# Attention and a look-up FFN on one core: context scaled by reciprocal sums instead of normalised probabilities, weights looked up bit by bit

## The reference

```
xn = layernorm(x)
q, k, v = split(xn @ qkv_w + qkv_b)                  # 16 heads of 128
scores = q @ k.T + alibi_mask                        # causal, slope 2**(-head/2), no 1/sqrt(d)
attn = softmax(scores);  ctx = attn @ v
attention = ctx @ out_w + out_b
gate, up = xn @ lut[gate_idx].T, xn @ lut[up_idx].T  # lut has 16 values, 688 x 256 codes each
ffn = (silu(gate) * up) @ lut[down_idx].T
out = x + attention + ffn
```

## Time and profile before

| | |
|---|---|
| median of three runs | 544.28 us (542.76 to 547.27) |
| the profiled execution: its own time | 543.26 us |
| its span (first to last instruction) | 541.5 us |
| mean granted TensorE clock | 0.987 of full speed |
| busy: PE / PEld / DVE / ACT / POOL | 493.8 / 422.4 / 414.2 / 360.9 / 403.6 us |
| one steady pair of heads | 57.0 us, six of them |
| last pair's end and FFN (from 440 us on) | 101.5 us |

### The profile page before, as it was taken

How to read it: one execution, slowest core, us unless ns; L and a number is a source line. 1 busy time by engine, 2 the same in 40 slices (tenths; PEclk the granted TensorE clock), 3 DMA queues, 4 the chain that set the end, 5 groups by cost and what they waited for, 6 DMA issues and landing times.

```text
span 541.5 us, 9700 instructions
## 1 busy us (share of the span) xinstructions
PE 493.8 (91%) x2826; PEld 422.4 (78%) x2826; DVE 414.2 (76%) x1067; ACT 360.9 (67%) x657; POOL 403.6 (75%) x312
## 2 busy tenths in 40 slices
PE   7896797999889988998899989997999989789998
PEld 6785576898779876987689768986798779578897
DVE  6796988788888878888788987888788886543541
ACT  3575867687767867595959685877678766824430
POOL 5533989788978998798969897889789979921400
PEclk9997999999999999999999999999999999979999
DMA  8204243332514070606160524134331514000001
GB/s 285 87 0 101 62 98 103 73 91 53 146 44 116 13 186 4 156 0 161 38 144 16 119 80 113 47 79 120 70 90 43 119 38 104 0 1 2 0 21 58
DMA packets 18948, 41.65 MB, mean 77 GB/s; under 512 B 4848, under 2 KB 7024, under 8 KB 18800
## 3 DMA queue, kind: packets, MB, share of 16 engines
q1 hardware_dynamic: 18928, 41.40, 30.2%
HBM read 11.83 MB, written 1.05 MB: 24 GB/s over the span
## 4 chain that ended last, share of the span: by engine, by line
POOL 44%; PE 23%; issue 21%; DVE 7%; ACT 3%; DMA 1%; POOLq 0%; DVEq 0%; ACTq 0%
POOL p_t_lo L1125 17%; POOL w_ffn L1153 15%; POOL work L1118 5%; PE ps_u L447 5%; PE ps_u L449 4%; PE ps_u L448 4%; DVE term L958 3%; PE ps_s L447 2%; PE ps_s L448 2%; PE ps_s L449 2%; POOL v_w_lo L1102 2%; POOL pad L1117 2%; POOL qk_w_lo L1097 2%; ACT ctx_t_hi L721 1%; DVE ctx_t_lo L898 1%
## 5 line engine op out<-in xcount | busy, mean ns | idle before, releaser
L1153 POOL TENSOR_TENSOR w_ffn<-w_ffn,term 128x1088 f32<-128x1088 f32 x60 | 155.0, 2584 | 45.4 <-DVE term L958 45.4
L1125 POOL TENSOR_TENSOR p_t_lo<-p_t_lo,p_t_hi 128x1024 fp32r<-128x1024 f32 (+2 forms) x60 | 133.1, 2251 | 0.0
L738 ACT ACTIVATE work<-work,neg_max 128x128 f32<-128x128 f32 (+7 forms) x128 | 99.0, 773 | 24.1 <-DVE neg_max L937 22.1
L937 DVE CUSTOM_DVE_ANT_0 work<-ps_s,alibi 128x128 f32<-128x128 f32 (+7 forms) x128 | 95.8, 749 | 0.0
L447 PE MATMUL ps_u<-p_t_hi,v_hi 128*128 128x512 f32 x192 | 70.5, 367 | 17.7 <-POOL p_t_lo L1125 17.4
L975 DVE STREAM_TRANSPOSE blocks<-work 128x512 f32<-128x512 f32 x120 | 65.3, 582 | 11.6 <-ACT work L750 11.6
L447 PE MATMUL ps_s<-k_hi,q_hi 128*128 128x256 f32 (+2 forms) x192 | 67.3, 350 | 5.3 <-DVE neg_max L937 5.3
L958 DVE TENSOR_SCALAR term<-codes,entry,table 128x1088 f32<-128x1088 uint8 x60 | 65.8, 1096 | 4.3 <-POOL w_ffn L1153 4.3
L449 PE MATMUL ps_u<-p_t_hi,v_lo 128*128 128x512 f32 x192 | 67.2, 350 | 0.0
L448 PE MATMUL ps_u<-p_t_lo,v_hi 128*128 128x512 f32 x192 | 67.0, 349 | 0.0
L448 PE MATMUL ps_s<-k_lo,q_hi 128*128 128x256 f32 (+2 forms) x192 | 65.8, 343 | 0.0
(11 more groups left out here) (148 smaller groups left out, 1271.1 us busy)
## 6 DMA issues: line engine op xcount, KB each, us to landing
p_t_lo<-blocks SPq DMA_DIRECT2D x240, 116.0 KB, 2.3
qk_raw<-w_qk SPq DMA_DIRECT2D x16, 256.0 KB, 2.7
w_ffn<-idx SPq DMA_DIRECT2D x1, 2176.0 KB, 11.0
v_raw<-w_v SPq DMA_DIRECT2D x8, 256.0 KB, 3.5
o_raw<-w_o SPq DMA_DIRECT2D x8, 256.0 KB, 2.9
out<-acc SPq DMA_DIRECT2D x8, 128.0 KB, 1.7
acc<-x SPq DMA_DIRECT2D x2, 256.0 KB, 3.0
acc<-x SPq DMA_DIRECT2D x1, 512.0 KB, 5.0
```

The source lines that it names most:

```text
L738: act.activation(slot(i), slot(i), ACT.Exp, bias=neg_max[:, col:col + 1], scale=-1.0, accum_out=row_sum[:, col:col + 1]).then_inc(exp_done, 1)
L937: dve.tensor_tensor_reduce(slot(i).rearrange("p (b c) -> p b c", b=banks), made_of, alibi[:, p, S - width:S].rearrange("p (b c) -> p b c", ...
L1125: pool.tensor_tensor(rows, rows.bitcast(F32), chunk_rows(0, chunk).bitcast(F32), ALU.subtract).then_inc(upper_lo, 1)
L1153: pool.tensor_tensor(piece, piece, term[:, :], ALU.add).then_inc(term_added, 1)
```

## The change

1. The probabilities stay unnormalised. `norm` is gone from ACT and POOL. DVE takes the reciprocals of four row sums at a time (`invert`, two per head instead of eight). SP writes these 128 x 4 numbers to a row of 512 in DRAM and reads the row back onto all 128 partitions (`send_inv`, `spread_inv`), twice a head. DVE multiplies the finished context by them (`scale`, in the place of its lo part), ACT then adds the bias and, in a second pass, makes hi, and POOL makes lo (`ctx_lo_of`).
2. The look-up works head by head on 272 codes (`PART`), all entries at once. DVE extracts four bits (`split_codes`, step 0). ACT fills a 128 x 8 x 272 buffer with the even table entries (`fill_codes`, end of step 0). DVE then picks with four predicated copies in steps 1 to 4, of 2176, 1088, 544 and 272 elements (`pick`), and ACT keeps the 272 results (`keep_codes`, step 5). POOL's sums are gone.
3. To make room, the weights of q and k have one buffer, and those of v and of the output share a raw one. The weights of the next head are now converted at step 2, after k1, and the units nk0 and nq0, which read them, go to steps 4 and 5. _out0 and _out1 go to 2 and 6.
4. The halving of the mask table goes from DVE (step 3) to POOL (step 5). The upper hi and lo parts start a step earlier (steps 3 and 4), and the upper blocks are turned one by one in steps 5 to 7. PE waits for `ctx_lo` before _out0 and _out2.

```diff
-QK_W_AT = 6
-V_W_AT = 2
+QK_W_AT = 2
+V_W_AT = 4
...
-ALIBI_AT = 3
...
+ALIBI_AT = 5
+HI_AT = {3: (0, 1), 4: (2, 3)}
...
     STEADY: [
-        (("q1", 0), ("k1", 1), ("nk0", 2), ("_out0", 3), ("nq0", 4), ("_out1", 5), ("_pv1-", 7), ("_pv1", 7),
+        (("q1", 0), ("k1", 1), ("_out0", 2), ("nk0", 4), ("nq0", 5), ("_out1", 6), ("_pv1-", 7), ("_pv1", 7),
          ("v0", 7), ("v1", 7)),
-        (("q1", 0), ("k1", 1), ("nk0", 2), ("_pv0", 2), ("v2", 3), ("nq0", 4), ("_out2", 4), ("v3", 5),
+        (("q1", 0), ("k1", 1), ("_pv0", 2), ("v2", 3), ("nk0", 4), ("_out2", 4), ("nq0", 5), ("v3", 5),
          ("_out3", 6), ("_pv1-", 7), ("_pv1", 7), ("pv0", 7)),
     ],
...
-        qk_w = [sb(f"qk_w_{s}", [P, 2, KT, 2 * D], F32R) for s in ("hi", "lo")]
+        qk_w = [sb(f"qk_w_{s}", [P, KT, 2 * D], F32R) for s in ("hi", "lo")]
...
+                sp.dma_start(inv_row[half].rearrange("(t q) -> q t", q=P),
+                             inv_sum[:, col:col + QT], allow_slow_non_contiguous=True).then_inc(inv_out, 16)
...
+                sp.dma_start(inv_rows[:, half, :], inv_row[half].partition_broadcast(P)).then_inc(inv_in, 16)
...
+            def upper_half(n, p):
+
+                send_inv(n, p, 1)
+                move(n, p)
+                spread_inv(n, p, 1)
...
                     if c == 0:
                         pe.wait_ge(o_w_hi, n)
                         pe.wait_ge(o_w_lo, n)
-                        pe.wait_ge(unit_used, number(n - 1, STEADY, 1, "pv0"))
+                        pe.wait_ge(ctx_lo, 16 * half_no(n - 1, 1, 0))
...
+                if "pv" in name:
+                    act.wait_ge(unit_used, no)
+                    rows = inv_rows[:, int(name[-1]), :]
+                    act.activation(rows, rows, ACT.Identity, bias=b).then_inc(ctx_biased, 1)
+                    act.wait_ge(ctx_biased, head)
+                    act.activation(unit_place(0, p, name), rows, ACT.Copy).then_inc(unit_hi, 1)
+                    return
...
+                evens = table[:, :].rearrange("p (c b) -> p c b", b=2)[:, :, 0:1]
+                act.activation(picked[:, :, :], evens.to_broadcast([P, PAIR_CODES, PART]),
+                               ACT.Copy).then_inc(codes_filled, 1)
...
+                        if i == 0:
+                            fill_codes(n, kind, p)
+                        if i == 5:
+                            keep_codes(n, p)
...
-                        if i == QK_W_AT and kind != LAST:
-                            act.wait_ge(qk_landed, n * 32 + (p + 3) * 16)
+                        if i == QK_W_AT and not (kind == LAST and p == 1):
+                            act.wait_ge(qk_landed, n * 32 + (p + 2) * 16)
                             act.wait_ge(unit_done, last_of(n, kind, p, "q1", "k1"))
...
+            def scale(n, p, name, bank, no, head):
+
+                c = int(name[-1])
+                dve.wait_ge(unit_done, no)
+                dve.wait_ge(inv_in, 16 * head)
+                dve.tensor_tensor(inv_rows[:, c, :], ps_u[:, bank, :], inv_rows[:, c, :],
+                                  ALU.mult).then_inc(unit_used, 1)
...
+                for bit in range(4):
+                    last = dve.tensor_scalar(bits[:, bit, :], codes, 1 << bit, None, ALU.bitwise_and)
+                last.then_inc(bits_made, 1)
...
+                count = PAIR_CODES // apart
+                dve.copy_predicated(out, bits[:, bit:bit + 1, :].to_broadcast([P, max(count, 1), PART]),
+                                    other).then_inc(codes_picked, 1)
...
+                        if i == 0:
+                            split_codes(n, kind, p)
+                        if 1 <= i <= 4:
+                            pick(n, kind, p, i - 1)
```

More of the change, by code:

```diff
@@ L340, in ffn_w @@
             if piece < 4:
[L341 removed]
+                room = (qk_w, v_w)[piece - 2][part]
+                return room[:, :, :].rearrange("p a b -> p (a b)")[:, in_piece:in_piece + width]
             in_piece += (piece - 4) * PIECE
@@ L386, in _, with send_inv, spread_inv @@
             sp.dma_start(bias[:, :, :], b_qkv).then_inc(bias_landed, 16)
[L387 removed]
+            sp.dma_start(vo_raw[:, :, :], w_v[0]).then_inc(v_landed, 16)
             sp.dma_start(table[:, :], lut.partition_broadcast(P)).then_inc(small_landed, 16)
[L389 removed]
+            sp.dma_start(out_bias(), b_out.partition_broadcast(P)).then_inc(small_landed, 16)
             sp.dma_start(w_ffn[:, :].bitcast(I32), idx).then_inc(idx_landed, 16)
[L391 to L395 removed]
+            sp.wait_ge(qk_w_hi, 1)
+            sp.wait_ge(qk_w_lo, 1)
+            sp.dma_start(qk_raw[:, :, :], w_qk[1]).then_inc(qk_landed, 16)
             sp.wait_ge(v_w_hi, 1)
             sp.wait_ge(v_w_lo, 1)
[L398 removed]
+            sp.dma_start(vo_raw[:, :, :], w_o[0]).then_inc(o_landed, 16)
+            def send_inv(n, p, half):
+                no = half_no(n, p, half)
+                before = 16 * no - 32
+                sp.wait_ge(inv_ready, no)
+                if not (isinstance(no, int) and no <= 2):
+                    sp.wait_ge(inv_in, before)
+                col = p * NT + half * QT
+                sp.dma_start(inv_row[half].rearrange("(t q) -> q t", q=P),
+                             inv_sum[:, col:col + QT], allow_slow_non_contiguous=True).then_inc(inv_out, 16)
+            def spread_inv(n, p, half):
+                no = half_no(n, p, half)
+                sent, before = 16 * no, 16 * no - 32
+                sp.wait_ge(inv_out, sent)
+                if not (isinstance(no, int) and no <= 2):
+                    sp.wait_ge(ctx_lo, before)
+                elif half == 1:
+                    sp.wait_ge(based, NT)
+                sp.dma_start(inv_rows[:, half, :], inv_row[half].partition_broadcast(P)).then_inc(inv_in, 16)
             def move(n, p):
@@ L667, in _ @@
                     if no in (0, 2):
-                        pe.wait_ge(unit_used, units)
+                        pe.wait_ge(ctx_lo, 16 * half_no(PAIRS - 1, 1, no // 2))
                     units += 1
@@ L836, in _ @@
                     if what == "pv":
-                        hi_of(PAIRS, 0, "_pv1", (units - 1) % 2, units)
+                        hi_of(PAIRS, 0, "_pv1", (units - 1) % 2, units, half_no(PAIRS - 1, 1, 1))
                         ffn_w_hi_of(4)
@@ L963, in invert, with turn_blocks @@
+            def invert(n, p, half):
+                dve.wait_ge(exp_done, tile_no(n, p, half * QT + QT - 1) + 1)
+                no = half_no(n, p, half)
+                if not (isinstance(no, int) and no <= 4):
+                    dve.wait_ge(inv_out, 16 * no - 64)
+                col = p * NT + half * QT
+                dve.reciprocal(inv_sum[:, col:col + QT], row_sum[:, col:col + QT]).then_inc(inv_ready, 1)
+            def turn_blocks(n, p, i):
                 dve.wait_ge(exp_done, tile_no(n, p, i) + 1)
-                col = (p * NT + i) % (2 * NT)
@@ L1011, in pair @@
                             if not (kind == FIRST and p == 0):
+                                if not kind == FIRST:
+                                    dve.wait_ge(ctx_lo, 16 * half_no(n - 1, p, 1))
                                 last = copy_bias(n, p, p, (2,))
@@ L1067, in _ @@
                     if what == "pv":
-                        lo_of(PAIRS, 0, "_pv1", (units - 1) % 2, number(PAIRS - 1, LAST, 1, "pv0", is_split) + 1)
+                        scale(PAIRS, 0, "_pv1", (units - 1) % 2, units, half_no(PAIRS - 1, 1, 1))
                     else:
@@ L1163, in _ @@
             all_pairs(pool, pair)
+            ctx_lo_of(PAIRS, 0, "_pv1", number(PAIRS - 1, LAST, 1, "pv0", is_split) + 1)
             for piece in range(4, PIECES):
```

272 lines of the change are left out of this document (135 added, 137 removed).

## The result

The changed kernel takes 624.29 us (median; 622.17 to 629.97) against 543.52 us (542.26 to 547.27) for the kernel before, measured beside it: ratio 1.149, 95% interval 1.139 to 1.158, slower by 81 us. The forecast was 571 us, the range ended at 600 us. The sign was right, the size was not.

A forecast was written before the change was run, and what follows sets the result against it. POOL was taken to cost PE 5.6 us a pair, all in p = 0. With new waits the halves came to 27.3 and 33.6 us, a pair 3.85 us more; seven pairs add 27 us to 543.26: 571 us, range 528 to 600.

The forecast's parts named there:

- The floor: PE's own work in a steady pair: 28.7 us in p = 1 plus 22.7 in p = 0, 51.4 against 57.05 us.
- Rival 3: Granted clock falls to 0.50 behind the wait before nk0: 584 us in one half a pair, 597 in both; chance 0.13.
- The waits: PE's new waits: 4.0 us before nk0 plus 0.8 for holds in p = 1, 4.1 plus 0.5 in p = 0.
- one chain per half: From q1's end through fill, k1, largest pick and mask 2 to nk0's weights: 11.4 us in p = 1, 10.2 in p = 0.
- Block move: Issue, landing, hi and lo parts before _pv1: 24 us in all, shorter than either half, so charged nothing.
- Fill 2.01 us: ACT's fill of 2176 elements at the end of step 0, priced by SBUF copies; bounds 1.0 and 2.4 us.
- Picks 4.84 us: DVE's four picks a head at the mask's 1.04 ns an element: 2.41, 1.28, 0.72 and 0.43 us; bounds half and twice.
- Bits 1.2 us: DVE's four bit extractions of 272 elements a head, 0.3 us each, from a range of 0.2 to 0.43.
- Shared path of DVE and POOL: POOL instructions under way hold DVE, near the picks of steps 3 and 4: 0.8 us in p = 1, 0.5 in p = 0.
- Scaling is cheap: Reciprocals' DMA round trip charged nothing, bounds 0 and 1 us a half; _out0's wait for `ctx_lo` covered by the longer chain.
- Order and single buffers as the costly part: Fill, largest pick and the next head's weights, now single-buffered, stand in the chain before nk0: PE waits 4.0 and 4.1 us.
- The forecast signs: In the changed profile: `qk_w_lo` waits about 4 us per half, POOL about 60% and DVE 76% busy, p = 1 longer by 6 us.

The follow-up runs named there:

- the weights at step 1: Changed kernel with the next head's q and k weights converted at step 1, behind exp 1, instead of step 2: 614.99 us, ratio 1.134.
- the fill a head earlier: Changed kernel with the look-up's fill moved from step 0 to step 5 of the head before, behind the copy that keeps the result: 630.76 us, ratio 1.163.
- the busy PE: Changed kernel with dummy transposes into free PSUM banks during PE's long waits before nk0, _out0 and scores 4: 618.45 us, ratio 1.140.
- the table of the hi parts: Upper hi parts back at steps 4 and 5: 535.92 us from 576.1 with scaling, new order and no look-up; 630.34 us in the changed kernel.
- the largest pick at the turn: Changed kernel with bits at step 6, fill at step 5 and the largest pick at step 0 between mask 0 and q_lo: 619.03 us, ratio 1.139.

## Why the prediction was wrong

**In numbers.** A steady pair was forecast at 60.9 us and is 68.1: 51.5 of PE's work and 9.4 of waits were forecast, 57.6 of busy PE and 10.6 of idle PE were measured. The gap of 7.2 us has three terms (rounded). Over the seven pairs' worth between the marks the time grew by 71.0 us where 27 were forecast, which is 44 us of the 53 missed. Most of the rest is the start, which took 7.0 us more where I allowed 3 either way. The sum was also put down unevenly: 27 us on 543.26 us are 570.3 and on the median 571.3, not 570.6, which changes nothing.

- *The floor, +1.2 us.* I subtracted 5.6 us of waits of the weight loads from the half p = 0 and called the remaining 22.7 us PE's work. But weight loads run beside matmuls: PE's own column in the earlier trace rows said 24.8 us busy, so only 3.5 us idle. The kernels without POOL's sums have PE busy for 52.6 to 53.0 us a pair. So POOL's relief was worth 1.8 us a pair, not 5.6. The row was in front of me; I took the wrong engine's waits.
- *The clock, most of +4.9 us of busy time.* Rival 3 with a chance of 0.13 is what the trace shows, in both halves of every pair: behind the wait of 3.2 us in p = 1 and that of 2.1 us in p = 0 the clock is at 0.50 for 5 to 6 us. The forecast had found the one row that showed it, and then trusted that the smaller waits of the earlier trace rows had left it at 1.00. Here waits of 2.69, 2.11 and 0.99 us follow each other within 11 us in p = 0, and one of 3.2 us stands in p = 1, where no wait of PE in the kernel before's steady pairs was over 1.5 us.
- *The waits, +1.2 us.* In p = 1 4.8 us for 4.0 + 0.8, right in sum. In p = 0 5.8 us for 4.1 + 0.5: the cover that I gave to _out0's wait for `ctx_lo` (2.69 us measured, "about 2 us" forecast) did not exist. It is followed by 2.11 us in front of scores 4 and 0.99 in front of nk0, because DVE is held by the same POOL instructions that PE waits for (the 3.06 us of the bits above).

**In causes.** These terms say where PE's time is, not what would give it back, and there the prediction failed more deeply. It had one chain per half. Each edit that took a link out of it, the weights at step 1, the fill a head earlier, the busy PE, won 0.5 to 1.8 us a pair, at most a third of what was expected: what replaced the wait were waits for DVE's results. That several chains end within a microsecond or two of each other is my reading of this. Of the 5.5 us a pair that the low clock was priced at, the busy PE gave back 1.9 in the half p = 1 and nothing in p = 0.

**Step by step.**

- Block move "charged nothing": right for _pv1, but the diff also moved ACT's passes over the moved blocks from step 4 to step 3, and I never asked who stands behind them in ACT's queue. With the scaling and without the look-up that is 40 us. In the changed kernel it is hidden behind the look-up's delay.
- Fill 2.01 us: 2.007. Picks 4.84 us a head by the mask's rate: 5.41 us where POOL is mostly elsewhere (the kernel before with the new look-up), 6.48 in the changed kernel. Bits 1.2 us a head: 1.04 and 1.98.
- Shared path of DVE and POOL, 0.8 and 0.5 us, at most 1.9 a pair: the two sums just given differ by 2.0 us a head, 4 us a pair. The rule of the Trainium skill that I weighed (SBUF — State Buffer, Who interferes with whom) is borne out for the picks, which read two inputs in SBUF (1.97 us for the smallest, below). The bits have one tensor input in SBUF and are held as well; the page allows this for a mode that the profile does not show.
- "Scaling is cheap", DMA included: right in the old order, 528.6 against 529.6 us. Its bound, that the small elements could hold back the block move, was put at 1 us a half; the move did land 2 to 5 us later, and what that costs in the new order is part of the 40 us.
- Order and single buffers as the costly part ("this decides"): half right. The single buffers cost nothing measurable, the order 47 us without a look-up; the new look-up costs 43 us alone and 51 us in the changed kernel.
- The forecast signs: waits for `qk_w_lo` "about 4 us each": 0.99 and 3.21 us. POOL at 60%: 42%. DVE at 76%: 73%. p = 1 longer by 6 us: 4.5.

**The loss, added up** along a path of kernels that differ by one part: old look-up removed, -14; scaling, -1; new order and steps, +47; single buffers, -3; new look-up, +51; together +80 of the 81 us measured. By another path the terms are others, as the table of the hi parts shows (40 us in one kernel, none in another).

**What stays open.** Which chains end last in the changed kernel is not settled. The run with the largest pick at the turn shows that it is not its place alone. The times rather fit a load of DVE in steps 0 to 4 together with the passage from head to head (pv0, scale, two ACT passes, q_hi), in which DVE is idle for 4.1 us in p = 0. But DVE is busy for only 77% of the time, so load alone is no proof. I did not try the passage by itself, nor the scaling with the new look-up in the old order, whose buffers would take 4 KB a partition more than those of the fullest kernel built here. The scaling with the hi parts early and no DMA of small elements is untested too.

## What to carry to other kernels

Take the floor of an engine from its own busy time, not from the waits of a unit that overlaps it. When a table of steps moves a pass one step earlier, look up what it waits for and what stands behind it in its queue, whatever the pass itself costs: here a one-line table was worth 40 us in one kernel. And when an order was balanced to a microsecond, a removed link can win a fraction of its length (here at most a third): price a new chain by the next two as well, and test it by removing one part at a time from both ends of the change, since the same edit gave 40 us at one end and none at the other.

## What the runs showed of the hardware

- A predicated copy with a byte mask and fp32 data costs 1.2 ns an element at 2176 (2.6 us), where the source is a repeated table entry, and 1.3 at 1088 (1.39 us), where it is not: the repeated source gains next to nothing.
- Small DVE instructions are held until a POOL instruction under way ends. In the changed kernel the smallest pick, 272 elements, took 0.52 us at 266.91, 0.2 us before the end of one of POOL's lo parts, and 1.97 us at 300.11: that lo part ran from 299.34 to 301.75, and the pick ended at 302.08. POOL is held as well. In the changed kernel with the weights at step 1 (DVE, then POOL), a lo part of 1.30 us took 3.36:

```profile
250.68 2.63 DVE L1041 COPY_PREDICATED picked<-bits,table 128x2176 f32<-128x2176 uint8 x1
251.06 3.36 POOL L1180 TENSOR_TENSOR qk_w_lo<-qk_raw,qk_w_hi 128x512 fp32r<-128x512 f32 x1 [6.18 <-issue]
```

- 512 numbers of 4 bytes from 128 partitions to DRAM take about 8 us until the next DMA, which waits for them, is issued. Kernel after, SP:

```profile
297.21 0.38 SPq L426 DMA_DIRECT2D inv_row<-inv_sum  x1
305.19 0.33 SPq L438 DMA_DIRECT2D inv_rows<-inv_row  x1
```

In the changed kernel DVE never waited for the rows that come back. Whether this DMA delays the block move behind it is open, as said above.
